# Turning every second pair of rows on VectorE and through DRAM, in the first and the last loop

## The reference

```
x = x + ffn_B(ffn_A(x, cond))             # 8 and 8 experts, 2 per token
x = x + ffn_D(attention(x, bias, mask))   # 16 experts, 2 per token

ffn_A: h = leaky(x @ w_gate[e]) * (x @ w_up[e]);        y = h @ w_down[e]   # + a shared expert
ffn_B: h = gelu(x @ W1[e] + b1[e]);                     y = h @ W2[e] + b2[e]
ffn_D: h = silu(x @ w1[e].T + b1[e]) * (x @ w3[e].T + b3[e]); y = h @ w2[e].T + b2[e]  # + a shared expert
```

## Time and profile before

| | |
|---|---|
| median of the runs | 781.69 us |
| profiled execution, its own time | 780.06 us |
| its span, first to last instruction | 778.2 us |
| granted TensorE clock, mean | 0.956 |
| busy, share of the span: TensorE, VectorE, ScalarE, POOL | 90%, 61%, 51%, 55% |
| first loop (A), first product of a pair | 45.0 to about 116 us |
| last loop (D), first product of a pair | 662.9 to about 746 us |
| last scatter of the last loop | 752.2 us |

### The profile page before, as it was taken

The page is one execution under the profiler, slowest core; times in us unless marked ns, Lnnn a source line. Parts: engine busy times, 40 slices in busy tenths (PEclk is TensorE's granted clock), DMA queues, the critical chain, the costliest instruction groups (busy, mean ns, idle before and its releaser), DMA issues. The chain is left out here.

```text
span 778.2 us, 15602 instructions
## 1 busy us (share of the span) xinstructions
PE 700.5 (90%) x4389; PEld 544.4 (70%) x4390; DVE 471.2 (61%) x1730; ACT 395.0 (51%) x1100; POOL 430.8 (55%) x540
## 2 busy tenths in 40 slices
PE   8878998675899999998799999899999989998986
PEld 5457995455699999986566666566666654887865
DVE  1722457267444445424888888899998945354546
ACT  4444651124344444424767657576766625765611
POOL 1075604560555685243876877898896654255550
PEclk9897999795699999999999999999999999999999
DMA  9834534345377777541899999888888773455428
GB/s 324 315 95 117 156 106 132 102 132 207 103 228 228 219 219 203 158 148 58 305 312 343 317 351 327 297 295 270 306 266 298 267 282 106 123 148 151 132 80 320
DMA packets 120813, 166.22 MB, mean 214 GB/s; under 512 B 29984, under 2 KB 97056, under 8 KB 119840
## 3 DMA queue, kind: packets, MB, share of 16 engines
q1 hardware_dynamic: 103632, 127.65, 49.3%
q0 software_dynamic: 10944, 30.03, 12.5%
q10 hardware_dynamic: 6160, 7.64, 3.0%
HBM read 100.07 MB, written 65.21 MB: 212 GB/s over the span
## 5 line engine op out<-in xcount | busy, mean ns | idle before, releaser
L1849 ACT ACTIVATE work<-work 128x129 f32<-128x129 f32 (+1 forms) x256 | 114.4, 448 | 73.7 <-DVE work L1986 72.6
L2011 DVE STREAM_TRANSPOSE region_bd<-work 128x384 f32<-128x384 f32 x128 | 73.1, 571 | 13.4 <-DMA c_blocks<-region_bd 9.3
L1430 POOL DMA_INDIRECT d_pairs<-work,home x47 | 47.6, 1012 | 52.5 <-DVE home_f L1180 35.3
L1595 PE MATMUL psY<-work,region_ac 128*128 128x256 f32 x256 | 70.0, 396 | 3.8 <-ACT work L1843 3.8
L2306 POOL TENSOR_TENSOR work<-region_bd,region_ac 128x386 f32<-128x386 f32 x64 | 59.6, 939 | 19.1 <-DVE work L1986 11.1
L1419 POOL DMA_INDIRECT b_pairs<-work,home x39 | 38.1, 976 | 56.7 <-DVE work L1124 54.6
L2306 POOL TENSOR_TENSOR work<-work,region_ac 128x386 f32<-128x386 f32 x64 | 59.6, 943 | 17.3 <-DVE work L1986 9.3
L1411 POOL DMA_INDIRECT work<-in_x,inv x39 | 37.2, 953 | 56.0 <-DVE inv L1337 36.0
L1633 PE MATMUL psM<-region_ac,work 128*128 128x256 f32 x256 | 66.9, 384 | 0.0
L1082 ACT ACTIVATE work<-work 128x512 f32<-128x512 f32 x39 | 24.6, 630 | 80.5 <-issue 46.9
L1622 PE MATMUL psL<-region_bd,work 128*64 128x256 f32 (+1 forms) x512 | 55.8, 338 | 7.2 <-DVE work L2020 3.9
(11 more groups left out here) (392 smaller groups left out, 1649.5 us busy)
## 6 DMA issues: line engine op xcount, KB each, us to landing
c_blocks<-region_bd SPq DMA_DIRECT2D x64, 512.0 KB
region_bd<-c_blocks SPq DMA_DIRECT2D x64, 512.0 KB
work<-d_rows SPq DMA_DIRECT2D x47, 132.0 KB
a_slots<-work SPq DMA_DIRECT2D x19, 256.0 KB
b_turned<-work SPq DMA_DIRECT2D x35, 128.0 KB
work<-b_turned SPq DMA_DIRECT2D x35, 128.0 KB
region_bd<-in_b_w SPq DMA_DIRECT2D x1, 3072.0 KB, 21.5
region_ac<-in_fside SPq DMA_DIRECT2D x12, 256.0 KB
```

Of the source, the lines that this page charges most:

```text
L1430: pool.indirect_dma_start(out=st.pair_dram, out_offset=bass.IndirectOffsetOnAxis(ap=home[:, t:t + 1], axis=0), in_=d_ys[:, t % ROWS, :], i ...
L1595: last = pe.matmul(psY[:, 0:SEQ], c_wq[:, c, j * P:(j + 1) * P], c_xnT[:, odd, c, :], start=(c == 0), stop=(c == KD - 1))
L1849: nc.scalar.activation(c_p[:, j % 2, o, a:z], c_sc[:, o, a:z], ACT.Exp, scale=-1.0, bias=c_min[:, o, i:i + 1], accum_out=c_sum[:, j % 2, o ...
L2011: nc.vector.transpose(out=c_x1[:, p % 2, :, (QT + 1) * o:(QT + 1) * (o + 1), :].rearrange("p b i q -> p i b q"), in_=c_p[:, j % 2, o, 1:1 ...
```

## The change

Pairs with an odd number from 5 up to the last but one are turned as the middle loop does it. For such a pair:

- TensorE leaves out `turn`, and ScalarE `copy_x`. The first product waits for a load and reads the rows in four pieces (`xTe`).
- VectorE makes two transposes in squares of 32 (`x_blocks`) in step p-4, behind `results`, into one of two buffers. In A the buffers lie in the region that holds gathered results later (`gat`), in D in the one for A's results (`ys`).
- SP stores the 256 KB of a pair (`sp_store_x`) and later loads them (`sp_load_x`). A store waits for the load of the exchanged pair before, a load for its store and for the first product three pairs before.
- The gathers of A and the row loads of D that reuse an exchanged pair's buffers wait for `x_blocks` in place of `turned`.

In A the store of pair p+6 and the load of pair p+5 follow the slot store of pair p on SP. In D they follow the row loads: after those of pair m comes the store of pair m-2 and the load of pair m-3. In D the ring of loaded rows has ten tiles in place of eight, and `homes` of pair p+1 stands ahead of `gated` of pair p (that of pair 0 ahead of the loop).

```
+ROWS_D = 10
+FIRST_EXCHANGED = 5
+EARLY = 4
...
+    def exchanged(self, p):
+
+        return p % 2 == 1 and FIRST_EXCHANGED <= p < self.outs - 1
...
+        xTe = xT.rearrange("p (r a i k q) -> p r a i k q", r=DEEP, a=4, i=PAIR, k=KD)
...
             def turn(p):
-                wait(pe, f.xT_ready, p - DEEP + 1)
+                wait(pe, f.xT_ready, f.by_pe(p - DEEP + 1))
...
             def products_in(p):
-                pe.wait_ge(f.xT_ready, p + 1)
+                if f.exchanged(p):
+                    wait_dma(pe, f.x_loaded, 0, f.ex(p))
+                else:
+                    pe.wait_ge(f.xT_ready, f.by_pe(p) + 1)
...
-                if p + 1 < f.outs:
+                if p + 1 < f.outs and not f.exchanged(p + 1):
                     turn(p + 1)
...
-                if f.st is A and p + 2 < f.outs:
+                if f.st is A and p + 2 < f.outs and not f.exchanged(p + 2):
                     copy_x(p + 2)
...
-                if f.st is D and p + 2 < f.outs:
+                if f.st is D and p + 2 < f.outs and not f.exchanged(p + 2):
                     copy_x(p + 2)
...
+            def x_blocks(p):
+
+
+                n = f.ex(p)
+                for t in f.tiles(p):
+                    dve.wait_ge(*rows_landed(f, 0, t))
+                if n >= 2:
+                    wait_dma(dve, f.x_stored, 0, n - 2)
+                for t in f.tiles(p):
+                    last = nc.vector.transpose(out=f.x1[:, n % 2, :, t % PAIR, :, :],
+                                               in_=slot_rows(f, t).rearrange("p (k q b) -> p b k q", k=KD, b=4))
+                last.then_inc(f.x_blocks, 1)
...
             fetch(0)
+            if f.st is D:
+                homes(0)
             for p in range(f.outs + f.behind):
                 if p < f.outs:
-                    if f.st is D:
-                        homes(p)
+                    if f.st is D and p + 1 < f.outs:
+                        homes(p + 1)
                     gated(p)
                 if p >= f.behind:
                     results(p - f.behind)
                 fetch(p + 1)
+                if f.exchanged(p + EARLY):
+                    x_blocks(p + EARLY)
...
                 elif st is A and t >= ROWS_DEEP:
-                    pool.wait_ge(f.turned, (t - ROWS_DEEP) // PAIR + 1)
+                    wait_rows_turned(pool, f, (t - ROWS_DEEP) // PAIR)
...
+        def sp_store_x(sp, f, p):
+
+
+            if f.exchanged(p):
+                n = f.ex(p)
+                sp.wait_ge(f.x_blocks, f.blocks_from + n + 1)
+                if n >= 1:
+                    wait_dma(sp, f.x_loaded, 0, n - 1)
+                sp.dma_start(f.x_dram[n % 2].rearrange("a (k b) m -> (a k) (b m)", b=4),
+                             f.x1[:, n % 2, :, :, :, :].rearrange("p b i k q -> p (b i k q)")).then_inc(f.x_stored.sems[0], 16)
+
+        def sp_load_x(sp, f, p):
+
+
+            if f.exchanged(p):
+                n = f.ex(p)
+                wait_dma(sp, f.x_stored, 0, n)
+                sp.wait_ge(f.h_mm, p - DEEP + 1)
+                sp.dma_start(xTe[:, p % DEEP, :, :, :, :].rearrange("p a i k q -> p a (i k q)"), f.x_dram[n % 2].rearrange("a s m -> s a m")
+                             ).then_inc(f.x_loaded.sems[0], 16)
...
-            for t in range(f.n):
-                if t >= ROWS:
-                    p = (t - ROWS) // PAIR
-                    sp.wait_ge(f.turned, p + 1)
-                    sp.wait_ge(st.homed, 2 * p + 2)
...
+            for m in range(f.outs + 2):
+                for t in f.tiles(m):
+                    if t >= ROWS_D:
+                        p = (t - ROWS_D) // PAIR
+                        wait_rows_turned(sp, f, p)
+                        sp.wait_ge(st.homed, 2 * p + 2)
...
+                sp_store_x(sp, f, m - 2)
+                sp_load_x(sp, f, m - 3)
...
+            sp_store_x(sp, f, FIRST_EXCHANGED)
             for p in range(f.outs):
                 n, at = len(f.tiles(p)), PAIR * (p % 2)
                 sp.wait_ge(f.y_out, p + 1)
                 sp.dma_start(tiles[:, PAIR * p:PAIR * p + n, :], ys[:, at:at + n, :]).then_inc(st.slots_stored.sems[p % RING], 16)
+                sp_store_x(sp, f, p + 6)
+                sp_load_x(sp, f, p + 5)
```

More of the change, by code:

```diff
@@ L165, in __init__ @@
         self.w_ready = sem(f"{name}_w_ready")
[L166 removed]
+        self.x_blocks, self.blocks_from = None, 0
         self.behind = 1 if kind == "silu" else 2
@@ L169, in __init__, with ex, by_pe @@
         self.y_out = sem(f"{name}_y_out")
+    def exchanged(self, p):
+        return p % 2 == 1 and FIRST_EXCHANGED <= p < self.outs - 1
+    def ex(self, p):
+        return sum(self.exchanged(q) for q in range(p))
+    def by_pe(self, p):
+        return max(p, 0) - self.ex(p)
 class Shared:
@@ L539, in build @@
         fB.w_ring, fB.w_of = b_wr, lambda e: one(b_w1, e)
+        fA.x1, fA.x_dram, fD.x1, fD.x_dram = a_x1, a_turned, d_x1, d_turned
+        fA.x_blocks = fB.x_blocks = fD.x_blocks = sem("x_blocks")
+        fB.blocks_from = fA.ex(fA.outs)
+        fD.blocks_from = fB.blocks_from + fB.n - TURNED
+        fA.x_stored, fA.x_loaded = (Use(RingOf((w1_loaded, r, r + 1)), fA.ex(fA.outs)) for r in range(2))
+        w1_loaded.count = fA.x_stored.after + fA.x_loaded.after + w1_loaded.count[2:4]
         fB.x_stored = Use(w1_loaded, fB.n - TURNED)
         fB.x_loaded = Use(slots_stored, fB.n - TURNED)
-        rows_loaded = RingOf((w1_loaded, 0, RING), (slots_stored, 0, RING))
-        fD.loaded = Use(rows_loaded, fD.n)
         D.slots_stored = Use(rows_gathered, fD.n)
@@ L901, in products_in @@
                         for k in range(KD):
-                            last = pe.matmul(pair_h[p % DEEP][:, t % PAIR, j, :], f.w_in(j, k, t), xT[:, p % DEEP, t % PAIR, k, :],
+                            rows_T = xTe[:, p % DEEP, :, t % PAIR, k, :] if f.exchanged(p) else xT[:, p % DEEP, t % PAIR, k, :]
+                            last = pe.matmul(pair_h[p % DEEP][:, t % PAIR, j, :], f.w_in(j, k, t), rows_T,
                                              start=(k == 0), stop=(k == KD - 1))
@@ L1392, in act_rows, with wait_rows_turned @@
                 nc.scalar.activation(quad, quad, ACT.Relu, scale=-1.0, bias=1.0).then_inc(st.eqrow_other, 1)
+        def wait_rows_turned(eng, f, p):
+            if f.exchanged(p):
+                eng.wait_ge(f.x_blocks, f.blocks_from + f.ex(p) + 1)
+            else:
+                eng.wait_ge(f.turned, f.by_pe(p) + 1)
         def pool_gather_rows(pool, st, first, last):
@@ L1576, in build @@
         tokens_stored.count = C.blocks_stored.after + C.blocks_loaded.after
+        rows_loaded = RingOf((w1_loaded, 0, RING), (slots_stored, 0, RING), (tokens_stored, 0, 2))
+        fD.loaded = Use(rows_loaded, fD.n)
+        fD.x_stored, fD.x_loaded = (Use(RingOf((tokens_stored, r, r + 1)), fD.ex(fD.outs)) for r in (2, 3))
+        tokens_stored.count = rows_loaded.count[8:10] + fD.x_stored.after + fD.x_loaded.after
         def pe_null(pe):
```

19 lines of the change are left out of this document (11 added, 8 removed).

## The result

The changed kernel is slower: 795.17 us median (790.77 to 799.64, 4 runs) against 782.00 (781.17 to 783.06, 4 runs) for the kernel before on the same chip, ratio 1.0168 with a 95% interval of 1.0109 to 1.0227. Its profiled execution took 794.43 us, of which the span is 792.7; before it was 780.06 and 778.2. Of the 14.5 us between the spans, the first loop, from its first product to its last second product, has 13.1 (87.3 instead of 74.2). The last loop, measured alike, gives 3.3 back (85.0 instead of 88.3), and the tail behind it takes 2.5 of that again (29.5 instead of 27.0). The start is 1.9 shorter.

A forecast was written before the change was run, and what follows sets the result against it. TensorE was taken to bound the first loop, and signals held behind four back-to-back scatters the last. 780.06 - 1.7 - 6 = 772.4, with 1.6 to the runs' median 774.0 us; eight in ten from 767.5 to 783.

The forecast's parts named there:

- The first loop's fixed sum: First loop: TensorE alone sets the pace, each pair costing 0.87 + 0.44 + 1.78 = 3.09 us.
- the worth of a turn: TensorE: each exchanged pair saves one turn of 0.44 us, at most 3.1 us in the first loop.
- the price of the exchange's transfers in the first loop: First loop, SP: a load of 2.95 us lands 0.4 us late, leaving a gain of 1.7 us.
- 256 KB to DRAM land within 2.22 us, which fits: First loop: the store ahead of each load lands within 2.22 us and adds nothing to the sum.
- That wait also moves the next load's deadline, so the mean is half: First loop: the 0.4 us wait counts as 0.2 us per exchanged product.
- The estimate of 2.6 us: First loop: load time by the Trainium skill, which would make the gain about 3 us instead of 1.7.
- The late load: Rival, chance 0.14: exchanged products wait for slow loads, first loop loses 4.1 us, last gains nothing; 785.8 us.
- The last loop's hold: Last loop: four back-to-back scatters delay other engines' signals; the exchange cuts the period from 7.47 to 6.58 us, gaining 6.
- The margin: Last loop: the even product's signal is out half a microsecond before the third scatter, ahead of the delay.
- Both gains arrive whole: End of kernel: closing loads wait for the last scatter, so the 1.7 and 6 us count in full.
- What is late next is POOL: Last loop: after the change POOL's four scatters and the signal delay come next as limit; no term in the sum.
- Costed at nothing: Ten buffers and earlier row ids cost nothing; VectorE's added transposes, 1.29 us in two pairs, stay below every forecast period.

The follow-up runs named there:

- e6: The changed kernel with the exchange kept only for pairs 13, 15 and 17 of the first loop; ratio 1.0069 to the kernel before.
- e1: The changed kernel with the exchange in the first loop alone, the last loop turning all pairs on TensorE; ratio 1.0153 to the kernel before.
- e5: Exchange in the first loop alone, transposes a pair earlier, store and load issued earlier, two exchanges in flight; ratio 1.0023 to the kernel before.
- e7: As e1, but POOL gathers 16 rows of a tile instead of 128 from the thirteenth tile on; ratio 1.0025 to the kernel before.
- e9: No exchange; two 128x128 additions on POOL after each pair's scatters from the last loop's eighth pair on; ratio 0.9997 to the kernel before.
- e16: No exchange; POOL additions of 128x64 and 128x32 after each pair's scatters from the last loop's fourth pair on; ratio 0.9929 to the kernel before.
- e17: As e16, with POOL additions of 128x128 and 128x64; ratio 0.9960 to the kernel before.
- e2: The changed kernel with the exchange in the last loop alone, the first loop as in the kernel before; ratio 0.9964 to the kernel before.
- e10: Exchange in the last loop alone, with transposes, store and load each one pair earlier; ratio 0.9980 to the kernel before.
- e3: The changed kernel with no pair exchanged; ten row buffers, earlier row ids and new DRAM tensors stay; ratio 0.9979 to the kernel before.
- e4: As e1, with separate semaphores for each DRAM buffer, so two exchanges can be in flight; ratio 1.0156 to the kernel before.

## Why the prediction was wrong, point by point

**The first loop's fixed sum** was right: 45.68 us between pairs 4 and 19 in every run without an exchange there. So was the worth of a turn: the step without a turn takes 2.65 us instead of 3.09 where no load is late (114.92 to 117.57), reading in four pieces costs nothing (1.95 us for sixteen matmuls), and the transposes take 0.59 us each instead of the 643 ns of the earlier trace rows.

**The step that failed is the price of the exchange's transfers in the first loop.** I took 2.95 us for the load from a line between two sizes, counted its lead from the slot store, and said of the store "256 KB to DRAM land within 2.22 us, which fits". The 2.22 us of the earlier trace rows are from 117 us, after the last gather. Among gathers a store takes up to 3.3 us (3.9 in e6, 4.4 in e1) and a load 4.1 to 6.2. The load may not start before the store has landed, so both errors add up: the wait of pair 7 is 3.46 us, where I had 0.4.

The store did not fit by the prediction's own rows either. Of the 9.70 us from product p to product p+4, it can start only when the transposes are through, and these stand behind the results of pair p-2: 4.08 + 1.29 = 5.37 us after product p. With its 2.22 it has landed at 7.59, where I let the load go out at 7.13. So 4.33 us were left for store and load, which need 2.22 + 2.95 = 5.17. The traces have the same lead: 73.32 to 77.66 for pair 7, and 90.45 to 94.72 for pair 13 of e6, with no exchange before it. By these rows the load is late, by an estimated 0.8 us, even where no gather is in flight; e5 gains by beginning a pair earlier.

"That wait also moves the next load's deadline, so the mean is half" made it smaller still. That a wait spares the next pair was right (pairs 9 and 15, each behind a long wait, wait for nothing); but the mean is 10.9 / 7 = 1.6 us. And a term was missing: behind a wait of 3.5 us TensorE ran its next products at the lower clock, which cost 4.4 us or more.

The Trainium skill (DMA: Bandwidth & Descriptors, Queues, rings and completion order) says that each DMA engine takes its queues in turn and goes on to the next only after a whole packet. That would make loads long beside gathers, and the trace's packet records fit it: 27 ns for the 512 B packets of the load, 161 in the median and 289 in the mean for the gathers' 4 KB ones, between 66 and 115 us. e7 fits too; no run here tells this rule from another way of sharing the engines. The estimate of 2.6 us that the prediction takes from the Trainium skill (DMA: Bandwidth & Descriptors, Anatomy of one DMA) goes by a fit that the section gives for transfers issued by GpSimd; after the last gather SP's stores land in 2.0 to 2.1 us here, its loads in 2.8 to 3.0.

**The late load** was one of my rivals, with 0.14 and 785.8 us. It came true in its place and for its reason, at three times its price (13.5 us in e1 instead of 4.1). Its upper end was the row of a 512 KB load from another stage; nothing in that price stood for the store before it or for the clock.

**The last loop's hold** was read rightly: e9, e16 and e17 take it away by a pause, and TensorE then runs at 3.09 us a pair. The margin was read too large: the product of the earlier trace rows ends at 700.23 (698.28 and 1.95), not at 700.06, where the next group starts, so some 0.36 us were left to the third scatter and not 0.5. What the exchange would do to the hold was wrong: the period fell to 7.23 us instead of 6.58. Some even products are ahead of the hold now, others are not (the earlier trace rows beside the period above), and exchanged products wait for late loads (two waits, 2.3 us, after; one of 0.7 in e2). The 5.1 and 1.9 us that the expectation of e10 puts to this are all idle time before first products, of every pair and cause. Take the waits away, and the hold takes their place (e10).

**"Both gains arrive whole"** failed. TensorE's loop is 3.3 us shorter, the last scatter 2.1 us earlier, the end of the span, counted from the loop's first product, 0.9; and 2.1 is no more than the traces without an exchange there differ by. "What is late next is POOL" was right and should have been a term: two scatters need 2.54 us of a pair, and in fours with a hold or in twos with a pause they come every 3.3 to 3.7 us. TensorE's pace hardly matters to them: 77.6 us or 87.4 for its loop, 90.4 or 91.1 for the last scatter. The earlier trace rows is also not the last scatter, as I called it here and in the table of the time before; two more follow, at 753.46 and 754.72.

**Costed at nothing and rightly so:** ten buffers, earlier row ids, the added VectorE work (39.41 of 60 us), ScalarE. e3 is within 0.5% of the kernel before.

## What to carry to other kernels

Price a transfer by a row from the stretch in which it will run, beside the same neighbours, and when it is two transfers in a row, add both and look at the lead before the bytes: the same exchange cost 13.5 us, or about nothing when it was begun a pair earlier. If the end of a loop is on another engine's path, shortening the engine that waits moves idle time only; ask what the last instruction waits for and price that engine's own pace first. A pause on a busy engine can give the others more than less work does, when its bursts hold them up: 10.7 us of TensorE's loop in e16, though the kernel's 0.7% there is explained only in part.

## What the runs showed of the hardware that was not expected

POOL's indirect transfers issued with 0.30 us between them, four in a row, hold up TensorE's signals: 5.1 to 5.8 us from the first of them to the gate behind. The semaphore records of the kernel before have it directly. The product of the earlier trace rows ends at 700.23 and its signal is recorded at 702.57; those of the second product and the turn behind it, which end at 701.09 and 701.53, at 703.32 and 703.38. That other engines' signals are held, as the prediction reads it, is not shown: in the same stretch VectorE's second instruction of `homes` starts 0.04 us after the end of the first, for whose signal it waits.

```profile
700.57 0.15 DVE L1180 TENSOR_TENSOR home_f<-work,inv_c 128x2 f32<-128x2 f32 x1
700.76 0.16 DVE L1182 SCALAR_TENSOR_TENSOR home<-home_f,inv_c 128x2 uint32<-128x2 f32 x1
```

With 0.59 us after every second transfer it is the same; with 1.10 us or more it is gone, and the 0.92 us of the earlier trace rows fit that. Whether POOL's issuing or the transfers in flight hold the signals, no run tells apart.

The start of the first loop may be a longer case. POOL issues gathers 0.30 us apart there until 62.06 us, and ScalarE copies rows that were turned by 53.92 only at 65.08; no run put a pause between those gathers.

```profile
65.08 0.59 ACT L1018 COPY work<-psX 128x512 f32<-128x512 f32 x1 [9.99 <-remote]
```

Indirect transfers of 16 rows cost POOL nearly what 128 do (837 ns against 953). After a wait of 3.46 us TensorE ran the next sixteen matmuls in 3.78 us instead of 1.95, and after waits of 2.87 to 4.36 us in e1, e4 and e6 in 3.17 to 3.78.
